# Preparing the fused weights inside the projection's program: an AdaLN attention and expert layer on one core

## The reference

```
mod = (silu(c) @ wmod).reshape(4, 6, 1, 256)         # rows sa, ca, ga, sb, cb, gb
ga, gb = sign(ga) * max(|ga|, 0.25), same for gb
h = layernorm(x) * (1 + ca) + sa
q_lat, k_lat, v_lat = h @ Wq_down, h @ Wk_down, h @ Wv_down    # 16 heads of 64 each
q, k = (q_lat @ Wq_up), (k_lat @ Wk_up)              # 16 per head, 8 of them with RoPE
v = v_lat @ Wv_up
x = x + ga * (softmax(causal(q k^T / 4)) v) @ Wc
h = layernorm(x) * (1 + cb) + sb
x = x + gb * experts(h)                              # top 2 of 8 FFN experts and 4 identities
```

## Time and profile before

| | us |
|---|---|
| median of 3 runs | 2914.22 (2913.52 to 2916.76) |
| profiled execution | 2915.7 |
| its span, first to last instruction | 2913.9 |

### The profile page before, as it was taken

How to read it: one execution, slowest core, us unless ns; L and a number is a source line. 1 busy time by engine, 2 the same in 40 slices (tenths; PEclk the granted TensorE clock), 3 DMA queues, 4 the chain that set the end, 5 groups by cost and what they waited for, 6 DMA issues and landing times. The chain is left out here.

```text
span 2913.9 us, 46074 instructions
## 1 busy us (share of the span) xinstructions
PE 2584.7 (89%) x16224; PEld 1334.0 (46%) x16225; DVE 1978.6 (68%) x2820; ACT 1498.4 (51%) x2726; POOL 713.8 (24%) x761
## 2 busy tenths in 40 slices
PE   6987289999999999999999999999576799898880
PEld 6554123333333333333333333332365688787770
DVE  4787398788788878878887887870364533565664
ACT  0566007777777777777777777778232311111110
POOL 0345401110110111011011101101247422573454
PEclk8999559999999999999999999999786899999995
DMA  3698922425623542562364144000673532453443
GB/s 105 172 249 231 153 58 68 73 63 114 121 38 91 125 65 71 115 121 37 93 125 74 62 65 71 13 9 16 174 215 132 204 99 95 143 165 111 131 136 124
DMA packets 243213, 315.40 MB, mean 108 GB/s; under 512 B 31312, under 2 KB 197728, under 8 KB 240736
## 3 DMA queue, kind: packets, MB, share of 16 engines
q1 hardware_dynamic: 202240, 244.70, 36.3%
q0 software_dynamic: 16896, 46.16, 5.1%
q10 hardware_dynamic: 23904, 22.29, 2.3%
HBM read 159.05 MB, written 153.22 MB: 107 GB/s over the span
## 5 line engine op out<-in xcount | busy, mean ns | idle before, releaser
L1039 DVE TENSOR_REDUCE mxc<-ps 128x2 f32<-128x1024 f32 (+4 forms) x1168 | 1298.2, 1148 | 315.0 <-PE ps L948 181.9
L1020 ACT ACTIVATE probs<-ps 128x512 f32<-128x512 f32 (+1 forms) x2240 | 1184.2, 587 | 401.2 <-PE ps L976 371.5
L948 PE MATMUL ps<-ks,qs 96*128 96x512 bf16 (+3 forms) x2560 | 696.6, 362 | 69.3 <-POOL ks L929 56.2
L976 PE MATMUL ps<-qs,ks 99*128 99x512 bf16 (+3 forms) x2560 | 736.3, 350 | 6.6 <-ACT probs L1020 4.2
L992 PE MATMUL ps<-probs,vs 128*32 128x512 f32 (+3 forms) x5120 | 600.0, 541 | 1.2 <-issue 0.5
L976 PEld LDWEIGHTS ps<-qs,ks 99*128 99x128 bf16 x2560 | 215.9, 97 | 606.9 <-ACT probs L1020 461.0
L919 POOL TENSOR_SCALAR_AFFINE_SELECT probs<-probs 128x512 f32<-128x512 f32 x256 | 162.3, 635 | 992.9 <-ACT probs L1020 992.9
L948 PEld LDWEIGHTS ps<-ks,qs 96*128 96x128 bf16 x2560 | 240.6, 99 | 283.0 <-DVE mxc L1039 61.8
L1588 ACT ACTIVATE hid_t<-ps 128x512 f32<-128x512 f32 x125 | 74.7, 597 | 473.0 <-PE ps L1561 473.0
L1561 PE MATMUL ps<-x_t,w_at 128*128 128x128 f32 x2000 | 262.6, 286 | 28.3 <-DVE w_at L1609 23.2
L1561 PEld LDWEIGHTS ps<-x_t,w_at 128*128 128x128 f32 x2000 | 242.0, 198 | 69.6 <-issue 40.8
(11 more groups left out here) (168 smaller groups left out, 1825.3 us busy)
## 6 DMA issues: line engine op xcount, KB each, us to landing
ks<-k_parts SPq DMA_DIRECT2D x96, 256.0 KB, 13.6
qs<-q_parts SPq DMA_DIRECT2D x96, 256.0 KB, 15.0
v_ones<-vout SPq DMA_DIRECT2D x64, 256.0 KB, 3.7
vs<-v_ones SPq DMA_DIRECT2D x16, 1024.0 KB, 26.8
attn_t<-o_sb SPq DMA_DIRECT2D x64, 256.0 KB, 3.1
xs<-slot_x SPq DMA_DIRECT2D x128, 128.0 KB, 2.0
slot_y<-ys ACTq DMA_DIRECT2D x122, 128.0 KB, 1.7
slot_x<-zero SPq DMA_DIRECT2D x24, 640.0 KB, 8.3
```

Source lines behind the costliest of these rows:

```text
L948: ins = pe.matmul(o[:, h, :], qs[r][0:SROWS, h0 + h, i * P:(i + 1) * P], ks[r][0:SROWS, h0 + h, 512 * c:512 * c + w], start=first, stop=no ...
L976: ins = pe.matmul(o[:, h, :], ks[r][0:SROWS + MROWS, h0 + h, j * P:(j + 1) * P], qs[r][0:SROWS + MROWS, h0 + h, J * QJ + lo:(J + 1) * QJ], ...
L1020: act.activation(probs[:, (NKT * r + m) % NPB, h0:h0 + nh, 0:QJ - lo], st_view(r, s), ACT.Exp, scale=DH ** -0.5).then_inc(exp_done, 1)
L1039: dve.tensor_reduce(mxc[:, h0:h0 + nh, i, c], red_view(u, at), AX_X, ALU.max).then_inc(red_done, 1)
```

## The change

The block setup is gone. Its work stands ahead of the first block of tokens in project's own programs, with these differences:

- Loads: SP's order is c, ident, gate, Wq_down, Wk_down, x of block 0, Wv_down, wmod, x of blocks 1 to 3, the small rest, the RoPE tables. ACT issues the ten up loads.
- The fused weights: the down weights are transposed as before, but now the up weights are the stationary operand (32 columns), so that a product gives 32 rows of the transposed fused weight. Four of these (`g`) go to four groups of 32 columns of PE. Four transposes per weight turn the result back (`turn_back`).
- Modulation: 6 products of 4 rows by 512 columns, in three column groups. sa and ca are transposed from there. The other four go through POOL on 4 partitions, and are stored to HBM by SP.
- In attention, SP loads Wc and ga (repeated over the partitions) behind the 24 row loads. POOL multiplies Wc by ga, before it fills `ks`. SP waits for this and loads the other rows.
- Buffers of the preparation lie in buffers that project and attention use later (`ks0`, `qs0`, `parts`, `vout`, `raw`).

```diff
...
+        down = [ks0[:, 0], ks0[:, 1], qs0[:, 0]]
+        down_t = parts[:, :, :, :, :, :].rearrange("p a b c d e -> p (a b c d e)").bitcast(F32).rearrange(
+            "p (x h c) -> p x h c", x=3, h=H // 2)
...
             def _(sp):
...
+                sp.dma_start(c_in[:, :], a["L0_c"]).then_inc(ld_c, 16)
+                sp.dma_start(k["ident"][:, :], a["ident"]).then_inc(ld_c, 16)
+                sp.dma_start(gate_in[:, :], a["L0_ffn_gate_w"]).then_inc(ld_c, 16)
+                first_down(0)
+                first_down(1)
+                first_x(0)
+                first_down(2)
+                sp.dma_start(wmod, a["L0_wmod"].rearrange("(c p) n -> p c n", p=P)).then_inc(ld_mod, 16)
+                for j in range(1, BPS):
+                    first_x(j)
...
+                sp.wait_ge(row_step, 2 * NROW - 1)
+                sp.dma_start(d["ga_rows"], rows[32:32 + B, 0:C]).then_inc(row_st, 16)
+                sp.dma_start(d["gb_rows"], rows[64:64 + B, C:2 * C]).then_inc(row_st, 16)
+                sp.dma_start(d["sbc_rows"][:, 0, :], rows[32:32 + B, C:2 * C]).then_inc(row_st, 16)
+                sp.dma_start(d["sbc_rows"][:, 1, :], rows[64:64 + B, 0:C]).then_inc(row_st, 16)
...
             @block.vector
...
+                turned_down(0)
+                turned_down(1)
+                fused(0)
+                back(0)
+                norm(0, 0)
+                norm_end(0, 0)
+                turned_down(2)
+                fused(1)
+                back(1)
+                fused(2)
+                back(2)
+                o = taken(U_MOD)
+                for g in range(3):
+                    ins = dve.tensor_copy(rows[32 * g:32 * g + B, :], o[32 * g:32 * g + B, :])
+                ins.then_inc(evac, 1)
...
+                dve.tensor_copy(k["mod"][:, :, :], o[:, 0:KC * B])
+                dve.tensor_scalar(k["ca1"][:, :, :], o[:, KC * B:2 * KC * B], 1.0, None, ALU.add).then_inc(evac, 1)
+                dve.tensor_copy(k["identb"][:, :], k["ident"][:, :])
+                staged(dve, (0, normed), (2, rotate), (3, split))
...
             @block.gpsimd
+                pool.wait_ge(pe_unit, U_MOD + 1)
                 pool.memset(vout[:, :, :, :, :], 1.0).then_inc(ones_done, 1)
+                pool.wait_ge(ones_done, 1)
+                pool.wait_ge(evac, U_MOD + 1)
+                apart(pool)
+                s = Steps(pool, row_step)
+                for p0, at in ((32, slice(0, C)), (64, slice(C, 2 * C))):
+                    g, sg = rows[p0:p0 + B, at], sgn[p0:p0 + B, at]
+                    s.link(pool.tensor_scalar(sg, g, 0.0, 2.0, ALU.is_ge, ALU.mult))
...
             @block.tensor
...
+                def fuse(x):
+                    if x == 0:
+                        pe.wait_ge(ld_up, 16 * 10)
+                    o = begin(U_FUSE[x])
+                    pe.wait_ge(evac, U_TURN[x] + H // 4)
+                    for u in range(2):
+                        for g in range(4):
+                            ins = pe.matmul(o[32 * g:32 * g + 32, u * C:(u + 1) * C], up[:, x, :], down_t[:, x, 4 * u + g, :],
+                                            start=True, stop=True)
+                    ins.then_inc(pe_unit, 1)
...
+                turn_down(0)
+                turn_down(1)
+                fuse(0)
+                turn_back(0)
+                turn_down(2)
+                fuse(1)
+                turn_back(1)
+                fuse(2)
+                turn_back(2)
+                o = begin(U_MOD)
+                pe.wait_ge(ld_mod, 16)
+                for c in range(KC):
+                    for g in range(3):
+                        ins = pe.matmul(o[32 * g:32 * g + B, :], c_t[:, c, :], wmod[:, c, 2 * C * g:2 * C * (g + 1)],
+                                        start=(c == 0), stop=(c == KC - 1))
...
+                pe.wait_ge(evac, NUNIT)
...
-def attention(nc, d, k, ps, g0, retired):
+def attention(nc, a, d, k, ps, g0, retired):
...
                 for n in range(1, R):
                     load(n, n)
+                for c in range(KC):
+                    rows = a["L0_attn_Wc"][c * P:(c + 1) * P, :].rearrange("(h d) n -> d h n", d=DH)
+                    sp.dma_start(k["wc"][:, 0, c, :], rows).then_inc(wc_ld, 16)
+                sp.dma_start(k["sbc"][:, :, 0, :], wide(d["ga_rows"][None, :, :], 0, P)).then_inc(wc_ld, 16)
                 for n in range(R):
                     load_v(n, n)
+                sp.wait_ge(wc_done, B)
+                sp.dma_start(k["sbc"][:, :, :, :], wide(d["sbc_rows"][None, :, :, :], 0, P)).then_inc(row_ld, 16)
+                sp.dma_start(k["gb"][:, :, :], wide(d["gb_rows"][None, :, :], 0, P)).then_inc(row_ld, 16)
                 maxima(0, 0)
...
             @block.gpsimd
...
+                pool.wait_ge(wc_ld, 16 * (KC + 1))
+                apart(pool)
+                for b in range(B - 1, -1, -1):
+                    ga = k["sbc"][:, b, 0, None, :]
+                    pool.tensor_tensor(k["wc"][:, b, :, :], k["wc"][:, 0, :, :], wide(ga, 1, KC), ALU.mult).then_inc(wc_done, 1)
+                pool.wait_ge(wc_done, B)
                 for r in range(R):
                     pool.memset(ks[r][SROWS:SROWS + MROWS, :, :], 1.0).then_inc(pool_init, 1)
                     pool.wait_ge(pool_init, r + 1)
```

More of the change, by code:

```diff
@@ L165, in build @@
             retired.append(g0["ld"])
[L166 to L170, removed]
+            project(nc, a, d, k, ps, g0, retired)
+            attention(nc, a, d, k, ps, g0, retired)
         with ExitStack() as c2:
@@ L503, in split, with normed, taken @@
                         dve.tensor_tensor(raw[:, par, x], raw[:, par, x], parts[:, par, 0, x], ALU.subtract).then_inc(sub_done, 1)
-                staged(dve, (0, norm), (0, norm_end), (2, rotate), (3, split))
+                def normed(b, j):
+                    if not (isinstance(b, int) and b == 0 and j == 0):
+                        norm(b, j)
+                        norm_end(b, j)
+                def taken(u):
+                    dve.wait_ge(pe_unit, u + 1)
+                    return bank(u)
@@ new lines, in turned_down, with fused, back @@
+                def turned_down(x):
+                    for pp in range(H // 4):
+                        dve.tensor_copy(down_t[:, x, 2 * pp:2 * pp + 2, :], taken(U_TURN[x] + pp)).then_inc(evac, 1)
+                def fused(x):
+                    dve.tensor_copy(w_t[:, x, :, :], taken(U_FUSE[x])).then_inc(evac, 1)
+                def back(x):
+                    o = taken(U_BACK[x])
+                    if x == 2:
+                        dve.tensor_copy(wf[:, 2, :, :], o).then_inc(evac, 1)
+                        return
+                    for c in range(KC):
+                        ins = dve.tensor_copy(wf[:, x, c, :].rearrange("p (e h d) -> p h e d", e=2, h=H),
+                                              o[:, c * C:(c + 1) * C].rearrange("p (h e d) -> p h e d", e=2, h=H))
+                    ins.then_inc(evac, 1)
@@ L510, in _ @@
+                s.link(pool.tensor_scalar(rows[64:64 + B, 0:C], rows[64:64 + B, 0:C], 1.0, None, ALU.add))
                 pool.wait_ge(tab_ld, 64)
@@ L568, in split @@
                         act.copy(parts[:, par, 1, x], raw[:, par, x]).then_inc(mid_done, 1)
+                act.wait_ge(up_zero, 1)
+                for x in range(3):
+                    for half in range(2):
+                        for n, name in enumerate(ups[x]):
+                            w = DH // len(ups[x])
+                            act.dma_start(up[half * L:(half + 1) * L, x, half * DH + n * w:half * DH + (n + 1) * w],
+                                          a[name]).then_inc(ld_up, 16)
+                act.wait_ge(ld_c, 16 * 3)
+                act.activation(c_sig[:, :], c_in[:, :], ACT.Sigmoid).then_inc(sig_done, 1)
                 staged(act, (0, norm), (1, modulate), (2, copies), (3, split), peeled=1)
@@ L598, in products, with begin, turn_down @@
                     ins.then_inc(v_done, 1)
+                def begin(u):
+                    if u >= 8:
+                        pe.wait_ge(evac, u - 7)
+                    return bank(u)
+                def turn_down(x):
+                    pe.wait_ge(ld_down[x], 16)
+                    for pp in range(H // 4):
+                        o = begin(U_TURN[x] + pp)
+                        for q in range(2):
+                            for c in range(KC):
+                                pair = 2 * pp + q
+                                ins = pe.transpose(o[:, (q * KC + c) * P:(q * KC + c + 1) * P],
+                                                   down[x][:, c, pair * P:(pair + 1) * P], k["ident"][:, :])
+                        ins.then_inc(pe_unit, 1)
@@ new lines, in turn_back @@
+                def turn_back(x):
+                    o = begin(U_BACK[x])
+                    pe.wait_ge(evac, U_FUSE[x] + 1)
+                    for c in range(KC):
+                        for u in range(2):
```

(14 more changed lines are left out.)

227 lines of the change are left out of this document (58 added, 169 removed).

## The result

The changed kernel takes 2945.4 us (median of 4 runs, 2936.8 to 2947.7) against 2914.9 before (4 runs): ratio 1.0099, 95% interval 1.0077 to 1.0121. It is 30.5 us slower; 29.5 was forecast. The profiled execution took 2947.65 us, with a span of 2945.9, which is 32.0 above that of before.

A forecast was written before the change was run, and what follows sets the result against it. The prediction took the time as a sum of stretches, each behind the last, with PE busy 1726 of 1800 us from 440 to 2240. 63.1 lost at attention's start minus 33.6 gained in preparation gave 29.5 us slower: 2944, range 2934 to 2957.

The forecast's parts named there:

- The preparation: Work ahead of the first tokens: one chain through DVE, norm of block 1 at 37.6 instead of 71.23, gaining 33.6 us.
- My last sum: End of the modulation: from 36.4, transposes and handoff 0.5 and three small copies 0.6, given as 37.6 us.
- The tables: In projection, RoPE of block 0 no longer waits for its tables: taken as 0 gain, 4 us at most.
- The seam: Start of attention: POOL's fills wait behind late loads and four products, so PE starts 63.1 us later after the block's start.
- rival 1: Start of attention: loads of Wc and ga pass the backlog, so the kernel is 8 us faster, 2907; chance 12%.
- One bound: Start of attention: copies of ga could land at 119 GB/s instead of 416, costing 4.5 us more.
- The shift passes on: Projection's waits are on each other, none on a fixed time, so all of it moves forward by 33.6 us.
- Rival 2: Preparation: PE's column groups run one after another, eight products cost 3.6 us, 7 us less gain, 2951; chance 6%.
- Rival 3: Projection is held by its stores, so the earlier start gains only a few us: 2970 or more; chance 2%.
- POOL's small operations: POOL's part of the modulation: eleven operations of 256 elements at 0.6 us each, hidden, ending near 45.

The follow-up runs named there:

- e5_tables_late: The changed kernel with the four loads of the RoPE tables issued behind the stores of the modulation rows: 2953.9 us (one run).
- e2_wc_early: The changed kernel with the loads of Wc and ga issued ahead of the 24 row loads, products still before the fills: 2932.4 us, ratio 0.9936 to the kernel before.
- e1: The changed kernel with POOL filling the three ks before it waits for Wc and ga and multiplies: 2920.7 us, ratio 0.9900 to the kernel before.
- e3: The kernel before with only the loads of Wc and four repeated rows, POOL's wait and four products added ahead of the fills: 3021.3 us, ratio 1.0233.
- e7: The kernel before with PE's wait for the fills moved to its first scores of group 0: 2927.1 us, ratio 0.9921.
- after_again: The changed kernel as it is, timed again on chip 1: 2985.0 us, ratio 1.0105 to the kernel before on that chip.

## Why the prediction was right

By its steps:

- **The preparation.** 33.6 us of gain forecast. At the norm of block 1 it is 71.23 - 38.29 = 32.9, at the first products 32.4. Two parts were off and nearly cancelled. I kept the gain at full clock because it was full in PE's first work, but from 26.8 to 35.3 us the granted clock was 0.50, the lower level: the modulation took 3.58 us on PE and not 1.8, and v's fused products 1.94. Against it, copies in a row were cheaper than I had them (v's four took 2.48 and not 3.4), so that DVE had v's last one done at 32.5, with 33.0 forecast. My last sum was off by 0.1 too: 36.4 + 0.5 + 0.6 is 37.5.
- **The tables.** I took 0 for the wait of RoPE that goes, 4 at most, since PE ran on beside it. It is 3.3 to 3.9: the lead was 33.0 us at the third block (67.91 against 100.93), 36.3 at the fourth (79.10 against 115.36) and 36.4 at the start of attention. PE did run on beside the wait, but DVE was late for the norm that the fourth block's transposes need: PE stood 2.33 us for it, and the transposes took 0.8 longer than they do in the changed kernel, about 3.1 in all. That such a wait comes on the path almost whole, e5_tables_late shows with 14.6 us for 16.5.
- **The seam.** 63.1 us forecast, 85.7 - 20.9 = 64.8 measured. Landing of ga: 58.2 forecast, 341.6 - 282.4 = 59.2. From there to the first product: 0 forecast, 0.6. Products: 4.7 forecast (4.9 with their waits), 4.92. Fills: the same. The loads landed in the order of their issue: the last row load at 339.3 (293.7 and the longest landing of `qs`, 45.6), Wc at 339.7 and 340.2, ga at 341.6. The step that carried it, that what is issued behind the row loads waits for all of them, is shown by e2_wc_early (7.3 us of landing in place of 40.1), and rival 1 has fallen. One bound was too wide: ga's 512 KB at 119 GB/s in place of 416 are 3.1 us more, not 4.5.
- **The shift passes on**, both ways and within 1.1 us: e1, e2, e3 and e7 move PE's start by -36.0, -20.2, +65.7 and -22.2 us, and the last scores by -34.9, -20.4, +65.8 and -21.8.
- **Rival 2** fell: eight products take 1.07 and not 3.6. **Rival 3** too: the start of attention moved by 36.4.
- **POOL's small operations** were forecast to end near 45 at 0.6 each. They took 0.72 to 1.10 and ended at 49.3, still ahead of the first RoPE at 53.7.

The net is 64.8 - 36.4 = 28.4 us (28.2 at the last scores), the forecast 29.5: the tables' gain of 3.3 to 3.9 that I left out was nearly balanced by the seam, which cost 1.7 more than I had, and the preparation, which gave 0.7 to 1.2 less. The measured 30.5 has 2.3 more behind the last scores, which no term of mine has and which the runs do not explain. Each term was off by 1 to 4 us; that 2944 and the measured 2945.4 agree within 1.4 is luck.

## What to carry to other kernels

Work taken off one path goes into some engine's queue, and there it stands in front of whatever that engine did next: look at who waits for the instruction behind it, and at what its own wait stands behind in the DMA queue. Here the same instructions, with three fills and one wait moved, made 2.8% (2900.2 against 2985.0 on one chip). An engine that runs on beside a wait does not prove the wait free; follow each of the others to the next thing it is late for.

## What the runs showed of the hardware

- SP issues more slowly behind a backlog: a load of 128 KB took 3.1 us to issue behind the row loads (6.16 for two) and 0.6 ahead of them (1.22 for two, in e2_wc_early).
- Row loads to 16 partitions kept the DMA engines at a share of 1.05 with 119 GB/s, 3.5 times less than loads to 128 partitions beside the same share.
- POOL took 1.07 to 1.10 us for a comparison and a product in one instruction (4 by 256 elements, one input), and 0.72 for a product of two inputs of the same size.
- The chips agree up to the last scores (before 2048.8, and 2046.9 on chip 11; after 2077.0, and 2076.5 on chip 1), and then not: from there to the end after_again took 899.9 us on chip 1 and e5_tables_late, of the same kind, 860.9 on chip 11.
